# Cross-attention with a dequantised feed-forward on one core: three local reorderings inside each step of the attention loop

## The reference, cut to what matters

```
def attention(query=layernorm(x), key=ctx, value=ctx):
    q = rope(query @ Wq);  k = rope(key @ Wk);  v = value @ Wv
    logits = einsum(q, k) * 0.0883883
    logits = 30 * tanh(logits / 30)
    logits = where(mask, logits, -1e30)
    weights = softmax(logits)
    return einsum(weights, v) @ Wo
x = x + attention(...)
h = silu(layernorm(x) @ dq(w1).T) * (layernorm(x) @ dq(w2).T)
x = x + h @ dq(w3).T
```

## Time and profile before

| | |
|---|---|
| median of 3 runs | 799.94 us (799.92 to 802.31) |
| the profiled execution's own time | 800.16 us |
| its span in the profile | 798.3 us |
| granted TensorE clock | 1.00 of full speed, all through |
| busy: PE / PEld / DVE / ACT / POOL | 99% / 80% / 83% / 69% / 46% of the span |
| chain that ended last | PE 85%, DVE 6%, issue 5%, ACT 2%, DMA 1% |

### The profile page before, as it was taken

One profiled execution on the slowest core, in us unless ns is written; L12 is line 12 of the kernel. 1 busy time (PEld: TensorE's weight loads), 2 busy tenths in 40 slices (PEclk: granted clock), 3 DMA queues, 4 the chain that ended last, 5 costly groups with the idle time before them and its releaser, 6 DMA issues.

```text
span 798.3 us, 10879 instructions
## 1 busy us (share of the span) xinstructions
PE 789.0 (99%) x3810; PEld 635.9 (80%) x3810; DVE 661.7 (83%) x741; ACT 547.4 (69%) x859; POOL 367.3 (46%) x210
## 2 busy tenths in 40 slices
PE   8999999999999999999999999999999999999998
PEld 6777887878887788878888888888778888888876
DVE  6897755898999999898988889899574999999913
ACT  6467737787877868678787788786643877868510
POOL 4773265446637457366465365473100534435010
PEclk9999999999999999999999999999999999999999
DMA  9636456333432433425235335231401031412022
GB/s 335 199 129 201 131 155 169 110 99 93 139 107 77 154 97 112 129 71 171 79 84 152 92 93 165 80 103 47 136 14 40 27 126 54 124 28 76 14 69 106
DMA packets 60981, 87.56 MB, mean 110 GB/s; under 512 B 6272, under 2 KB 29952, under 8 KB 60928
## 3 DMA queue, kind: packets, MB, share of 16 engines
q1 hardware_dynamic: 59744, 84.06, 35.7%
q10 hardware_dynamic: 1184, 2.82, 1.0%
HBM read 51.00 MB, written 19.07 MB: 88 GB/s over the span
## 4 chain that ended last, share of the span: by engine, by line
PE 85%; DVE 6%; issue 5%; ACT 2%; DMA 1%; POOL 0%; POOLq 0%; SPq 0%; DVEq 0%
PE bank L530 7%; PE prjs L514 7%; PE prjs L516 7%; PE bank L532 7%; PE bank L531 7%; PE prjs L515 7%; PE bank L590 7%; PE avp L618 6%; PE trp L503 4%; PE bank L496 3%; PE bank L498 3%; PE bank L497 3%; PE prjs L498 2%; PE prjs L496 2%; PE prjs L497 2%
## 5 line engine op out<-in xcount | busy, mean ns | idle before, releaser
L1294 POOL TENSOR_TENSOR qT<-cs_loop,sw 128x512 f32<-128x512 f32 x56 | 107.2, 1915 | 183.4 <-DMA sw<-cs_loop 176.1
L514 PE MATMUL prjs<-xh,wqh 128*128 128x512 f32 x256 | 123.3, 482 | 0.0
L530 PE MATMUL bank<-woh,ath 128*128 128x512 f32 x256 | 100.8, 394 | 1.0 <-DVE atl L1161 0.9
L516 PE MATMUL prjs<-xh,wql 128*128 128x512 f32 x256 | 100.2, 391 | 0.0
L532 PE MATMUL bank<-woh,atl 128*128 128x512 f32 x256 | 99.9, 390 | 0.0
L531 PE MATMUL bank<-wol,ath 128*128 128x512 f32 x256 | 99.7, 389 | 0.0
L862 ACT ACTIVATE ath<-trp 128x512 fp32r<-128x512 f32 x64 | 38.2, 596 | 89.5 <-PE trp L503 89.5
L515 PE MATMUL prjs<-xl,wqh 128*128 128x512 f32 x256 | 99.5, 389 | 0.0
L995 DVE TENSOR_TENSOR cs_loop<-prjs,csq 128x1024 f32<-128x1024 f32 x56 | 68.3, 1220 | 21.4 <-PE prjs L516 21.2
L987 DVE SCALAR_TENSOR_TENSOR nfv<-nfq,nfv 128x1408 f32<-128x1408 uint8 x42 | 79.1, 1883 | 0.2
L850 ACT ACTIVATE nrm<-avp,rs 128x128 f32<-128x128 f32 x256 | 72.6, 372 | 7.0 <-DVE rs L1148 6.7
(11 more groups left out here) (187 smaller groups left out, 1966.6 us busy)
## 6 DMA issues: line engine op xcount, KB each, us to landing
sw<-cs_loop SPq DMA_DIRECT2D x112, 128.0 KB, 2.3
stage<-wq_pieces SPq DMA_DIRECT2D x32, 256.0 KB, 2.9
stage<-wo_pieces SPq DMA_DIRECT2D x32, 256.0 KB, 3.1
stage<-dq_scratch SPq DMA_DIRECT2D x32, 256.0 KB, 3.2
ks_scratch<-qT SPq DMA_DIRECT2D x16, 256.0 KB, 3.1
vs_scratch<-vst SPq DMA_DIRECT2D x16, 256.0 KB, 3.5
kcur<-ks_scratch SPq DMA_DIRECT2D x16, 256.0 KB, 2.9
vcur<-vs_scratch SPq DMA_DIRECT2D x16, 256.0 KB, 3.4
```

Of the source, the lines that this page charges most:

```text
L514: nc.tensor.matmul(o, wqh[:, g, k, :], xh[:, k, cs], start=k == 0, stop=False)
L516: last = nc.tensor.matmul(o, wql[:, g, k, :], xh[:, k, cs], start=False, stop=k == KT - 1)
L530: nc.tensor.matmul(o, ah, wh[:, g, :], start=g == 0, stop=False)
L1294: nc.gpsimd.tensor_tensor(dst, products(ru, slot)[:, 0, :], sw[:, slot, :], ALU.add).then_inc(roped, 1)
```

## The change

On each of three engines, one pair of neighbours inside the step changes places. TensorE does the query unit j+8 ahead of the logits of step j+3. ScalarE does `values(j+1)`, then `high(34+j)`, then `weights(j+3)`. VectorE does `rope_parts` of unit j+8 ahead of `mask(j+3)`. No instruction is added or removed, GpSimd's and SyncE's programs are as before, and no buffer or semaphore changes.

```diff
@@ TensorE, head
                     if j + 1 < NSTEP:
                         weighted_values(j + 1)
+                    if j + AHEAD < NUNIT:
+                        q_unit(j + AHEAD)
                     if j + 3 < NSTEP:
                         logits(j + 3)
-                    if j + AHEAD < NUNIT:
-                        q_unit(j + AHEAD)
@@ ScalarE, head
                     for c, i in signs[0:1]:
                         nf_above_bound(c, i)
+                    if j + 1 < NSTEP:
+                        values(j + 1)
+                    if j + 2 < 8 * NKV - 8:
+                        high(34 + j)
                     if j + 3 < NSTEP:
                         weights(j + 3)
-                    if j + 2 < 8 * NKV - 8:
-                        high(34 + j)
-                    if j + 1 < NSTEP:
-                        values(j + 1)
@@ VectorE, head
                     for c in nf_prepares(j):
                         nf_prepare(c)
-                    if j + 3 < NSTEP:
-                        mask(j + 3)
                     u = j + AHEAD
                     if u < NUNIT:
                         rope_parts(NK + u, u % 2, csq[:, :, :])
+                    if j + 3 < NSTEP:
+                        mask(j + 3)
                     for c, i in adds[between:]:
                         nf_add(c, i)
```

## The result

The changed kernel takes 831.7 us (median of 4 runs, 830.37 to 834.26) against 800.35 us before (4 runs): a ratio of 1.0392, 95% interval 1.0376 to 1.0408. Slower, as forecast, but by 31 us where I had said 15; 831.7 lies above my range of 802 to 828.

What follows compares the result with a forecast made beforehand. TensorE was taken as the bound at 7.66 us a step; a ring of 7.72 plus 0.49 blocking made two-add steps 8.21, stalls 17.0 in place of 2.10, so 800.16 + 14.9 = 815.1, called 815 us; range 802 to 828.

Steps and rivals of the forecast that it cites:

- TensorE as the bound, 56 steps of 7.66 us: Loop before the change: TensorE hardly ever starves, 56 x 7.66 = 428.96 of 431.06 us, only 2.10 us stalls.
- I take 0 for the swap, bounds 0.02: TensorE's swap of query unit and logits costs 0, within 0.02 us per step either way (1 us).
- The ring: VectorE's and ScalarE's in-order queues, mask product to mask product, once per step: 7.72 us with two adds, against TensorE's 7.66.
- The blocked add: GpSimd's rope arrives within the end add and blocks the next step's first add on VectorE: 0.49 us per two-add step.
- The sum over the loop: Steps of each kind added up, less what was in hand: +17.0 us of TensorE stalls in place of 2.10, so +14.9.
- +7.6: GpSimd's normalise and rescale block an add or push weight_low into one, steps 6, 14, 23, 28, 43: 7.6 us, bounds 0 and 11.
- Rival 3: Rope arrives during add_out, or weight_low gets ahead of an add: 0.34 us more in 38 steps, +13, 828 us; chance 0.11.
- Steps 56 to 63: hidden, at 0 (bounds -0.5 to +0.5): Last eight steps, without adds, rope or high part: ring of 4.14 us hidden behind TensorE's 4.93, cost 0.
- Step 0's 0.95: Step 0's stall, logits waiting for a mask product: the query unit now covers it, 0.95 us won.
- Rival 1: Two-add steps: ring closes within a step, rope doesn't block, only step 0's 0.95 is won: 799.2 us; chance 0.11.
- Where TensorE would wait: Some 17 us of TensorE waiting at L530 for atl; waits at L503, L590 or L514 would prove the forecast wrong.

Runs made afterwards that it cites:

- end add moved: The whole change, with VectorE's adds at the step's end moved ahead of the mask product, behind rope_parts: 807.06 us, ratio 1.0085.
- rope held: The whole change, with GpSimd's rope of unit j+8 held by a wait until the next step's first add is done: 820.24 us, ratio 1.0250.

## Why the prediction was wrong, point by point

- **TensorE as the bound, 56 steps of 7.66 us: right** for before. (The step of 304.56 to 312.22, called 22 in the earlier trace rows, is step 23, the one of the earlier trace rows; nothing in the sum hangs on that.) **"I take 0 for the swap, bounds 0.02": wrong in size.** A step without a stall is 0.05 to 0.07 longer. It matters little here, as few steps have no stall, but 56 x 0.07 = 3.9 is most of the loop's excess with the end add moved (435.10 - 428.96 = 6.1).
- **The ring: right, and shown** by putting rope_parts into it (9.0), taking the blocking out (7.87) and taking the end add out (807 us). My terms sum to 7.72; the trace has 7.87. The mask product lets the next add in after 0.61 and not the 0.54 that I took from a row where a reciprocal follows it; exp to mask product is 0.61, not exp's own 0.58; tanh is 0.65 and the scalings 1.01. These 0.15 recur in every round without a collision.
- **The blocked add: right**, 0.51 for 0.49 by the rows, and GpSimd's rope arrives where I said (284.26 - 279.98 = 4.28 for 4.32). It lets go as the add does, as I took it from the earlier trace rows: 285.71 + 2.13 - 1.61 = 286.23 against a rope that ends at 286.36. The Trainium skill has a blocked operation wait until about 115 ns after VectorE's end (SBUF — State Buffer, "A bandwidth-pool intuition that's wrong", on a DMA whose descriptors GpSimd writes). This trace doesn't agree for two compute operations: here too the blocked one starts 0.13 ahead of the other's recorded end.
- **The sum over the loop: the mis-sized term.** Predicted 17.0 of stalls, measured 459.38 - 428.96 = 30.4, so 13.4 short. Adding up the rounds of each kind, reciprocal to reciprocal: 28 plain two-add steps took 237.2 for 28 x 8.21 = 229.9, +7.3, of which 20 rounds at 8.38 or 8.39 make 3.6, and steps 1, 3, 45, 48 and 52 at 8.9 to 9.6 most of the rest; five two-add steps behind a prepare took 46.4 for 43.1, +3.4 (steps 21, 35 and 50 are 9.45 to 9.51, where I let GpSimd's normalise pass free); two three-add steps with a chunk's first add +1.6; all other kinds together +1.2. That is +13.5. The failed step is thus the ring's sum together with "+7.6" for collisions. Against the rounds that recur undisturbed (8.39 blocked, 7.87 not), the ring was short by 0.15 to 0.18 in some 50 rounds, about 8.5 of the 13.5. Collisions came to about 14.2, over the stated upper bound of 11 and 6.6 over the term; three two-add rounds that the rope didn't block (steps 16, 32 and 54, 7.86 to 7.87) gave 1.6 back.
- **Rival 3, a dearer block,** happened, in some eight rounds and not in all: in steps 3, 45 and 48 the rope arrives during add_out and the first add takes 2.65 to 2.73; in steps 21, 35, 50 and 52 weight_low, pushed back by a normalise or rescale, gets ahead of the end add (2.68 to 2.73), and the rope behind it takes its 0.5 from the first add as well.
- **"Steps 56 to 63: hidden, at 0 (bounds -0.5 to +0.5)": wrong, by 4.2 us,** of which 1.1 is the loop's lateness in step 56 and some 3 their own order. I summed VectorE's queue behind the mask product without the layer norm's work, which takes the adds' place there from step 58 on. The run with the change in these steps alone shows it.
- **Step 0's 0.95:** in the profile its spacing is 7.76, so 0.85 is won; by itself it can't be measured.
- **Rival 1 (no slower)** would have needed rounds of 7.66 on average. With the rope's blocking taken out of most rounds the kernel still stood at 820.
- **Where TensorE would wait: right.** 29 of the 30.4 us stand at L530, and none of note at L503, L590 or L514.

Of the profiled excess, 834.26 - 800.16 = 34.1, the loop makes 28.3, the last eight steps 4.2, the start's variation 1.5.

## What to carry to other kernels

Before moving work ahead of other work in an in-order queue, ask whether the moved work waits for another engine, and whether that engine has something queued behind the result of what was passed over: if both hold, a ring closes, and its full length, every queued operation included, competes with the bound engine's step. Sum such a ring from spacings of the same pairs of neighbours, since 0.15 us per round over 50 rounds is 7.5 us, and sum it again for the iterations at the end, where other work fills the same places. A reordering also shifts where deadlines stand: the late logits here cost by themselves, but gave the mask product room that a later edit depended on.

## What the runs showed of the hardware that was not expected

- TensorE's twelve matmuls of 512 columns start a little further apart where they follow the logits (L590) or the weighted values (L618) than where they follow another unit of twelve. From the second to the twelfth start the query unit takes 2.29 and the output unit 2.27 before (step 23), and 2.31 and 2.30 in the step at 259.25 with the end add moved. With the logits between the two units none follows the other, and unstalled steps are 7.69 to 7.74 and not 7.66. Why the spacing differs stays open.
- When an add and GpSimd's next operation both wait for the GpSimd operation that runs, the add goes first: 78 times in the six traces read for it (before, the whole change, ScalarE's part, TensorE's and VectorE's parts, end add moved, rope held), and never the other way. So it is add_out, which GpSimd doesn't block, that lets the rope in between two adds.
- Seven of the traces have a TensorE wait of 2.33 to 2.37 us at the output unit in step 61. In two of them (end add moved, ScalarE's and VectorE's parts) the granted clock behind it is 0.50 for some 3 us, in the other five it stays at 1.00. Why it falls in these two and not in the others no run here shows; where it does, the same wait costs 1 us more.
- The L987 adds of the loop lose time to GpSimd in every kernel (record over 1.61 us, summed where it is more than 0.2): 21 us before the change, 30 after it, 38 with the end adds in the gap, 19 with the rope held, and only 7 with ScalarE's part alone, the slowest kernel. The clearest pair is TensorE's part alone, 10 us, and with VectorE's part, 63 us: both kernels take 820 to 821. The time lost to blocking says nothing of the kernel's time until it is known which adds lie in the chain.
